# The closing phase of a fused attention and mixture-of-experts kernel: eight buffers, all loads issued at the start, four neighbouring tokens to a partition, the sum in place

## The chip, the cores and the metric

The kernel runs on one core of one Trainium2 chip. The metric is the device time of one execution in microseconds (us), the median of several. A core has four compute engines that matter here: TensorE (PE, matrix products), VectorE (DVE), ScalarE (ACT) and GpSimd (POOL). SyncE (SP) issues most of the transfers, which 16 DMA engines carry out between the large memory (DRAM) and the on-chip memory of 128 partitions (SBUF). Engines run on their own and wait for each other at semaphores: an instruction or a finished transfer raises one, and another engine waits until it has a given value. All data is float32.

## The reference

Only the last lines matter for the change. `D` is 256; there are 2 x 2048 = 4096 tokens.

```python
def _layernorm(x, axis=-1, eps=1e-05):
    m = jnp.mean(x, axis=axis, keepdims=True)
    v = jnp.var(x, axis=axis, keepdims=True)
    return (x - m) / jnp.sqrt(v + eps)
...
    x = L0_attn_x
    x = _layernorm(x + _L0_attn_ref(x, ...), axis=-1)   # gated delta rule over 16 heads
    x = _layernorm(x + _L0_ffn_ref(x, ...), axis=-1)    # 6 of 64 experts, and a shared one
    return x
```

## The kernel before

The program is a row of phases, each a block of its own with a barrier at its end: `gates_phase` and `delta_phase` (the attention), `mix_phase` (output projection, first normalisation, routing, the shared expert), `expert_phase` (64 experts), and `combine_phase`, the only one that the diff touches.

The experts' results stand in two DRAM tensors, `acc[0]` and `acc[1]`, each of 128 + 4096 rows of 256 numbers. The first 128 rows are for unused slots; the other rows belong to the tokens. `acc[0]` starts from the residual plus the shared expert's output; the even experts add into `acc[0]` and the odd ones into `acc[1]`. `combine_phase` computes, for each token, the sum of its two rows and the normalisation of that sum, and stores it to `out`. It moves 2 x 4 MiB in and 4 MiB out.

It works in eight groups (`GROUPS` = 8) of 512 tokens. For each group:

- SP loads the group's rows of `acc[0]` into `first` and of `acc[1]` into `second` (lines 1432 and 1433), 512 KB each. In SBUF a group is 128 partitions x 1024 numbers.
- DVE adds the two (line 1452) and takes mean and variance of each token (`bn_stats`, line 1455, and `bn_aggr`, line 1458, four of each, since a partition holds four tokens).
- POOL makes from these the scale and the shift in four small operations on 128 x 4 numbers (lines 1467, 1469, 1470 and 1473; line 1469 is a power of -1/2, called the power operation below).
- ACT applies them, four activations of 128 x 256 (line 1483), into `res`.
- SP stores `res` (line 1441).

Each of `first`, `second`, `total` and `res` has two buffers; group `g` uses number `g % 2`. So DVE waits with group `g` until ACT has finished group `g - 2` (`done`), ACT waits until the store of group `g - 2` has landed (`stored`), and SP issues the loads of group `g + 2` only when DVE has summed group `g` (`summed`). SP's own order is written out by hand: the loads of groups 0 and 1; then for each group `g` the loads of group `g + 2`, and after them the wait for `done` of group `g` and its store. The loads of a later group thus stand behind the store, and behind the wait, of an earlier one.

`rows` sets which tokens a partition holds: token `g*512 + k*128 + p` in place `k` of partition `p`. A transfer of a group is 512 runs of 1 KB.

`gates_phase`, at the program's start, has transfers of the two kinds that the change makes: it loads its input in eight pieces of 128 partitions x 1024 numbers, runs of 4 KB, each with a semaphore of its own (`gates_xs`, line 82), for the first of which TensorE waits (line 121); and it stores zeros to `acc[1]` in runs of 8.25 KB (line 95).

`s.w13`, named by the change, is the on-chip store for expert weights (28 x 704 numbers on a partition), last read by `expert_phase`.

Of the kernel before, what the change touches and what calls it, by code (L numbers as in the profile page):

```python
# [15 lines left out]
NTILE = NTOK // 128  # L16
# [14 lines left out]
EPS = 1e-5  # L31
# [1377 lines left out]
def combine_phase(nc, a, s, out):  # L1409

    sem = s.sem
    with ExitStack() as own:  # L1412
        def two(name, cols):
            return [own.enter_context(nc.sbuf_tensor(f"combine_{name}{i}", [128, cols], F32)) for i in range(2)]

        first, second, total, res = two("first", 1024), two("second", 1024), two("total", 1024), two("res", 1024)
        st, mv, rstd, shift = two("st", 24), two("mv", 8), two("rstd", 4), two("shift", 4)
        loaded, stored = [sem(f"c_loaded{i}") for i in range(2)], [sem(f"c_stored{i}") for i in range(2)]
        summed, st_out, mv_out, eps, power, mean, shifted, done = (
            sem(f"c_{n}") for n in ("summed", "st_out", "mv_out", "eps", "power", "mean", "shifted", "done"))  # L1420
        GROUPS = NTILE // 4
# [24 lines left out]
        def _(ve):  # L1446
            for g in range(GROUPS):
                e = g % 2
                ve.wait_ge(loaded[e], 32 * (g // 2 + 1))
                if g >= 2:  # L1450
                    ve.wait_ge(done, 4 * (g - 1))
                ve.tensor_tensor(total[e][:, :], first[e][:, :], second[e][:, :], ALU.add).then_inc(summed, 1)  # L1452
                ve.wait_ge(summed, g + 1)
                for k in range(4):
                    ve.bn_stats(st[e][:, k * 6:k * 6 + 6], total[e][:, k * D:k * D + D]).then_inc(st_out, 1)  # L1455
                for k in range(4):
                    ve.wait_ge(st_out, 4 * g + k + 1)
                    ve.bn_aggr(mv[e][:, k * 2:k * 2 + 2], st[e][:, k * 6:k * 6 + 6]).then_inc(mv_out, 1)  # L1458

        @block.gpsimd  # L1460
        def _(po):
            for g in range(GROUPS):
                e = g % 2
# [3 lines left out]
                po.tensor_scalar(rstd[e][:, :], view(mv[e], 1, (2, 4)), EPS, None, ALU.add).then_inc(eps, 1)  # L1467
                po.wait_ge(eps, g + 1)
                po.tensor_tensor(rstd[e][:, :], rstd[e][:, :], view(s.minus_half, 0, (0, 4)), ALU.pow).then_inc(power, 1)  # L1469
                po.tensor_scalar(shift[e][:, :], view(mv[e], 0, (2, 4)), -1.0, None, ALU.mult).then_inc(mean, 1)  # L1470
                po.wait_ge(power, g + 1)
                po.wait_ge(mean, g + 1)
                po.tensor_tensor(shift[e][:, :], shift[e][:, :], rstd[e][:, :], ALU.mult).then_inc(shifted, 1)  # L1473

        @block.scalar
        def _(ac):
            for g in range(GROUPS):
                e = g % 2
                ac.wait_ge(shifted, g + 1)
                if g >= 2:  # L1480
                    ac.wait_ge(stored[e], 16 * (g // 2))
                for k in range(4):
                    ac.activation(res[e][:, k * D:k * D + D], total[e][:, k * D:k * D + D], ACT.Identity,  # L1483
                                  bias=shift[e][:, k:k + 1], scale=rstd[e][:, k:k + 1]).then_inc(done, 1)


def program(nc, a, out):
    with ExitStack() as ctx:
# [32 lines left out]
        mix_phase(nc, a, s)  # L1521
        expert_phase(nc, a, s)
        combine_phase(nc, a, s, out)


# [89 lines left out]
```

## Time and profile before

| | |
|---|---|
| Time, median of 3 runs | 1837.96 us (1837.03 to 1841.89) |
| The profiled execution's own time | 1834.91 us |
| Its span, first to last instruction | 1833.0 us |
| Busy over the span | PE 88%, DVE 65%, ACT 50%, POOL 47% |
| `combine_phase` in it | from 1781.46 us (first load issued) to 1833.0 us |
| Busy from 1781 to 1833 us | DVE 23.28, ACT 16.58, POOL 15.99, PE 0 us |
| DMA in that stretch | 12.58 MB, mean 242 GB/s, engines busy 74% |

The shares of the whole span are those of the long phases before. For the change only the last 52 us count: there no engine is busy for even half of the time, and the DMA engines for three quarters of it. Lines of the trace give a start in us from the span's start and a duration; `[... <-X]` says how long the engine sat idle before and what ended that.

### The profile page before, as it was taken

What the parts mean: (1) busy time and instruction counts of PE and PEld (TensorE: products, weight loads), DVE (VectorE), ACT (ScalarE), POOL (GpSimd) and SP (SyncE); (2) the same over time, 40 slices, a digit from 0 to 9 for tenths busy, and PEclk for the clock granted to TensorE, in tenths of its full rate; (3) what the DMA queues carried; (4) which work ended last, traced back from release to release, by engine and by line L of the source; (5) the groups of instructions that cost most, each with busy time, mean ns of one, the idle gap of its engine ahead of it and who ended that gap; (6) DMA issues with size and microseconds to landing.
All of it is one profiled execution on the core that took longest, in us unless ns stands there. A gap on an engine that the chain in (4) does not pass through costs nothing. (4 is left out here: it accounts for less than half of the span.)

```text
span 1833.0 us, 74029 instructions
## 1 busy us (share of the span) xinstructions
PE 1616.1 (88%) x31244; PEld 1234.2 (67%) x31244; DVE 1194.4 (65%) x3029; ACT 909.6 (50%) x2314; POOL 865.8 (47%) x1133
## 2 busy tenths in 40 slices
PE   7479999999999999999999999759999994899950
PEld 6136666666676666667667666658888884878840
DVE  1378888888888888888888888514555553222215
ACT  1266766676676666666666666311222221333313
POOL 0034344344344344344344344214777776677853
PEclk9799999999999999999999999879999998899985
DMA  6235455556555555555555555434555551799557
GB/s 272 81 80 119 113 115 121 126 113 124 126 114 121 126 114 122 126 113 123 126 113 122 115 115 118 80 106 149 176 153 176 153 153 35 203 262 223 93 93 244
DMA packets 530218, 245.45 MB, mean 134 GB/s; under 512 B 423504, under 2 KB 497872, under 8 KB 528992
## 3 DMA queue, kind: packets, MB, share of 16 engines
q1 hardware_dynamic: 377824, 200.75, 42.1%
q10 hardware_dynamic: 133632, 20.98, 6.1%
q0 software_dynamic: 18432, 18.99, 5.9%
q8 instruction: 247, 4.05, 1.0%
q14 instruction: 83, 0.68, 0.1%
HBM read 169.29 MB, written 71.37 MB: 131 GB/s over the span
## 5 line engine op out<-in xcount | busy, mean ns | idle before, releaser
L375 PE MATMUL delta_p_j<-delta_xt,delta_w 128*128 128x512 f32 x768 | 386.2, 626 | 31.4 <-DMA delta_xt<-in_xt 17.5
L575 DVE SCALAR_TENSOR_TENSOR delta_kq<-delta_hist,cw,delta_kq 128x512 f32<-128x512 f32 x384 | 295.6, 770 | 30.7 <-ACT delta_kq L723 23.7
L716 ACT ACTIVATE delta_hist<-delta_p_j 128x512 f32<-128x512 f32 x192 | 114.8, 598 | 251.9 <-PE delta_p_j L375 248.0
L889 POOL TENSOR_TENSOR delta_sd<-state,eg_end 128x256 f32<-128x256 f32 x128 | 104.4, 815 | 283.2 <-DVE state L655 283.2
L375 PEld LDWEIGHTS delta_p_j<-delta_xt,delta_w 128*128 128x128 f32 x768 | 131.5, 191 | 146.6 <-issue 111.9
L1248 POOL DMA_INDIRECT slot_tokens<-mix_tokens,mix_slot x192 | 190.2, 990 | 62.4 <-issue 61.8
L436 PEld LDWEIGHTS delta_p_i<-delta_kkq,rt 64*64 64x64 f32 x4096 | 130.3, 135 | 73.1 <-DVE delta_kkq L639 67.9
L864 POOL TENSOR_SCALAR delta_n<-delta_n 128x8 f32<-128x8 f32 x64 | 15.5, 242 | 296.7 <-DVE delta_n L606 296.7
L436 PE MATMUL delta_p_i<-delta_kkq,rt 64*64 64x32 f32 (+1 forms) x4096 | 143.3, 214 | 13.9 <-DVE delta_kkq L639 13.5
L1371 DVE SCALAR_TENSOR_TENSOR expert_gate<-expert_gate,expert_p_h 88x256 f32<-88x256 f32 x64 | 26.7, 417 | 174.7 <-ACT expert_gate L1391 174.7
L589 DVE SCALAR_TENSOR_TENSOR delta_yv<-delta_hist,cw,delta_yv 128x512 f32<-128x512 f32 x128 | 132.5, 1035 | 8.1 <-ACT delta_yv L723 5.9
L1342 PE MATMUL expert_p_h<-expert_xbt,w 128*88 128x128 f32 x1024 | 127.3, 278 | 9.9 <-ACT expert_xbt L1385 9.0
L779 ACT ACTIVATE delta_kpv<-delta_kpv,delta_root 128x64 f32<-128x64 f32 x512 | 135.4, 346 | 0.0
L1342 PEld LDWEIGHTS expert_p_h<-expert_xbt,w 128*88 128x88 f32 x1024 | 115.6, 158 | 29.2 <-ACT expert_xbt L1385 27.5
L883 POOL TENSOR_TENSOR delta_root<-delta_n,half_power 128x8 f32<-128x8 f32 x64 | 133.9, 2093 | 0.0
L495 PEld LDWEIGHTS delta_p_c<-delta_r,delta_kkq 64*64 64x64 f32 x2048 | 71.0, 136 | 92.4 <-issue 86.4
L1036 PE MATMUL mix_p_y<-mix_wo,mix_ot 128*128 128x256 f32 x512 | 117.9, 384 | 14.8 <-DMA mix_wo<-in_wo 14.8
L773 ACT ACTIVATE delta_kpv<-delta_kpv,delta_fk 128x64 f32<-128x64 f32 x512 | 128.8, 343 | 0.5 <-POOL delta_fk L871 0.5
L647 DVE TENSOR_TENSOR delta_r<-delta_kpv,delta_p_c 128x256 f32<-128x256 f32 x128 | 53.8, 420 | 98.1 <-PE delta_p_c L470 97.1
L1310 POOL DMA_INDIRECT acc<-expert_yb,expert_tokens x64 | 100.6, 1572 | 32.2 <-ACT expert_yb L1397 17.7
L1036 PEld LDWEIGHTS mix_p_y<-mix_wo,mix_ot 128*128 128x128 f32 x512 | 96.2, 193 | 27.0 <-issue 14.9
L632 DVE TENSOR_TENSOR delta_xi<-delta_xi,delta_outer 128x15 f32<-128x15 f32 (+7 forms) x480 | 99.0, 206 | 16.4
(145 smaller groups left out, 3641.4 us busy)
## 6 DMA issues: line engine op xcount, KB each, us to landing
delta_xd<-x_scratch SPq DMA_DIRECT2D x256, 128.0 KB, 4.3
delta_w<-in_wqkv SPq DMA_DIRECT2D x64, 416.0 KB
w<-in_w SPq DMA_DIRECT2D x64, 352.0 KB
delta_eg<-eg_rows SPq DMA_DIRECT2D x128, 130.0 KB
n_scratch<-delta_kkq ACTq DMA_DIRECT2D x128, 128.0 KB
mix_ot<-ot SPq DMA_DIRECT2D x16, 1024.0 KB, 5.7
w<-in_w SPq DMA_DIRECT2D x64, 176.0 KB
ot<-delta_o SPq DMA_DIRECT2D x32, 256.0 KB
```

The source lines that it names most:

```text
L375: mm = pe.matmul(p_j[:, :], w[e][:, (ch * 3 + n) * 128:(ch * 3 + n) * 128 + 128], xt[m // 8 % 2][:, ch * 512:ch * 512 + 512], start=ch == ...
L436: mm = pe.matmul(view(p_i, g * C + first, (1, count), parts=half(sh)), view(lhs, g * C, (1, C), parts=half(sh)), view(rhs, at + g * C + fi ...
L575: ve.scalar_tensor_tensor(out, view(hist[e], i * 2 * 518 + tap, (259, 2), (1, 256)), cw[:, column:column + 1], out, ALU.mult, ALU.add).the ...
L589: ve.scalar_tensor_tensor(out, view(hist[e], 518 + tap, (259, 2), (1, 256)), cw[:, column:column + 1], out, ALU.mult, ALU.add).then_inc(co ...
L716: ac.activation(view(hist[e], n * 518 + 3, (259, 2), (1, 256)), p_j[:, :], ACT.Copy)
L773: ac.activation(kpv[:, at:at + C], kpv[:, at:at + C], ACT.Copy, scale=fk[:, g:g + 1]).then_inc(kp_out, 1)
L779: ac.activation(kpv[:, at:at + C], kpv[:, at:at + C], ACT.Copy, scale=root[:, g:g + 1]).then_inc(vp_out, 1)
L883: po.tensor_tensor(root[:, :], n2[:, :], view(s.half_power, 0, (0, 8)), ALU.pow).then_inc(small, 1)
L889: po.tensor_tensor(view(sd, 0, (128, 2), (C, 2), (1, C)), view(state, first_pair(group) * 128, (C, 2), (128, 2), (1, C)), view(s.eg_end, g ...
L1036: mm = pe.matmul(p_y[i % 2][:, 0:D], ot[i // 2 % 2][:, p * 256 + i % 2 * 128:p * 256 + i % 2 * 128 + 128], wo[:, p * D:p * D + D], start=p ...
L1248: po.indirect_dma_start(out=s.tok.ap(), out_offset=bass.IndirectOffsetOnAxis(ap=slot[i % 2][:, k:k + 1], axis=0), in_=tokens[:, i:i + 1], ...
L1342: mm = pe.matmul(p_h[e % 2][0:HALF, piece * 128:piece * 128 + 128], s.w13[:, at * 704 + ch * SI + piece * HALF:at * 704 + ch * SI + piece ...
```

## The change

Every group has a place of its own, so nothing is reused within the phase. Eight stretches of `s.w13` take the loads of `acc[0]` and then the sums (`total`). Eight `res` buffers take the loads of `acc[1]` and, once the sum is made, the results. DVE adds in place. `first` and `second` are gone, and with them the waits for `summed` (SP), `done` (DVE and POOL) and `stored` (ACT). SP issues all 16 loads first and then the eight stores, each behind its wait. `rows` now puts tokens `g*512 + 4p` to `g*512 + 4p + 3` on partition `p`, so that a transfer is 128 runs of 4 KB.

```diff
-        first, second, total, res = two("first", 1024), two("second", 1024), two("total", 1024), two("res", 1024)
-        st, mv, rstd, shift = two("st", 24), two("mv", 8), two("rstd", 4), two("shift", 4)
-        loaded, stored = [sem(f"c_loaded{i}") for i in range(2)], [sem(f"c_stored{i}") for i in range(2)]
+        total, res = [s.w13[:, g * 1024:g * 1024 + 1024] for g in range(GROUPS)], each("res", 1024)
+        st, mv, rstd, shift = each("st", 24), each("mv", 8), each("rstd", 4), each("shift", 4)
+        loaded, stored = [sem(f"c_loaded{i}") for i in range(GROUPS)], sem("c_stored")
...
         def rows(t, g, skip):
-            return bass.AP(t, (g * 4 + skip) * 128 * D, [[D, 128], [128 * D, 4], [1, D]])
+            return bass.AP(t, (g * 4 + skip) * 128 * D, [[4 * D, 128], [1, 4 * D]])
...
-            def load(g):
-                if g >= 2:
-                    sp.wait_ge(summed, g - 1)
-                sp.dma_start(view(first[g % 2], 0, (D, 4), (1, D)), rows(s.acc[0], g, 1)).then_inc(loaded[g % 2], 16)
-                sp.dma_start(view(second[g % 2], 0, (D, 4), (1, D)), rows(s.acc[1], g, 1)).then_inc(loaded[g % 2], 16)
-
-            load(0)
-            load(1)
             for g in range(GROUPS):
-                if g + 2 < GROUPS:
-                    load(g + 2)
+                sp.dma_start(total[g], rows(s.acc[0], g, 1)).then_inc(loaded[g], 16)
+                sp.dma_start(res[g][:, :], rows(s.acc[1], g, 1)).then_inc(loaded[g], 16)
+            for g in range(GROUPS):
                 sp.wait_ge(done, 4 * g + 4)
-                sp.dma_start(rows(out, g, 0), view(res[g % 2], 0, (D, 4), (1, D))).then_inc(stored[g % 2], 16)
-            for i in range(2):
-                sp.wait_ge(stored[i], 16 * GROUPS // 2)
+                sp.dma_start(rows(out, g, 0), res[g][:, :]).then_inc(stored, 16)
+            sp.wait_ge(stored, 16 * GROUPS)
...
-                e = g % 2
-                ve.wait_ge(loaded[e], 32 * (g // 2 + 1))
-                if g >= 2:
-                    ve.wait_ge(done, 4 * (g - 1))
-                ve.tensor_tensor(total[e][:, :], first[e][:, :], second[e][:, :], ALU.add).then_inc(summed, 1)
+                ve.wait_ge(loaded[g], 32)
+                ve.tensor_tensor(total[g], total[g], res[g][:, :], ALU.add).then_inc(summed, 1)
...
                 po.wait_ge(mv_out, 4 * g + 4)
-                if g >= 2:
-                    po.wait_ge(done, 4 * (g - 1))
...
                 ac.wait_ge(shifted, g + 1)
-                if g >= 2:
-                    ac.wait_ge(stored[e], 16 * (g // 2))
```

POOL's and ACT's operations are otherwise the same, on `[g]` in place of `[e]`.

On SP's queue, at the start of the phase, this is the order of the transfers with the semaphores that each waits for (`c_summed` is DVE's sum, `c_done` ACT's last activation; `w` is the stretch of `s.w13`):

```order
-L1432 DMA combine_first<-acc 128x4x256
-L1433 DMA combine_second<-acc 128x4x256
-L1432 DMA combine_first<-acc 128x4x256
-L1433 DMA combine_second<-acc 128x4x256
-L1432 DMA combine_first<-acc 128x4x256 [waits c_summed]
-L1433 DMA combine_second<-acc 128x4x256
-L1441 DMA out<-combine_res 128x4x256 [waits c_done]
...
+L1431 DMA w<-acc 128x1024
+L1432 DMA combine_res<-acc 128x1024
...
+L1435 DMA out<-combine_res 128x1024 [waits c_done] x8
```

The pair of loads in the new order stands eight times, with no wait and no store between; the stores, which stood between the loads, have moved behind the last load.

On DVE, from the third group on (group 2), this is the sum and the statistics, before and now:

```order
-L1452 TENSOR_TENSOR combine_total<-combine_first,combine_second 128x1024 [waits c_done,c_loaded0]
-L1455 BN_STATS combine_st<-combine_total 128x6 [waits c_summed]
-L1455 BN_STATS combine_st<-combine_total 128x6 x3
-L1458 BN_AGGR combine_mv<-combine_st 128x2 [waits c_st_out] x4
...
+L1442 TENSOR_TENSOR w<-w,combine_res 128x1024 [waits c_loaded2]
+L1445 BN_STATS combine_st<-w 128x6 [waits c_summed]
+L1445 BN_STATS combine_st<-w 128x6 x3
+L1448 BN_AGGR combine_mv<-combine_st 128x2 [waits c_st_out] x4
```

The operations and their shapes stand as they were; the wait for ACT (`c_done`) is gone, and the load has a semaphore of its own.

## Rows read from the trace of the kernel before

**Rows 1.** Busy time by stretch: time, engines busy, TensorE clock, DMA share, GB/s.

```profile
1781.00:1833.00 52.00, 0.00 (x0) 0.00 (x0) 23.28 (x72) 16.58 (x32) 15.99 (x32) 0.50 0.74 242
```

**Rows 2.** The group of DVE's sums, from 1781 us: busy, mean ns, idle before and releasers.

```profile
L1452 DVE TENSOR_TENSOR combine_total<-combine_first,combine_second 128x1024 f32<-128x1024 f32 x8 | 9.8, 1225 | 35.0 <-DMA combine_second<-acc 29.9 <-ACT combine_res L1483 5.2
```

**Rows 3.** Chain that ended last, in order of time, from 1781 us.

```profile
1782.98 7.84 DMA combine_second<-acc
...
1799.50 7.93 DMA combine_second<-acc
...
1816.35 5.83 DMA combine_second<-acc
```

**Rows 4.** DVE in order of time, from 1781 us.

```profile
1787.37 1.22 DVE L1452 TENSOR_TENSOR combine_total<-combine_first,combine_second 128x1024 f32<-128x1024 f32 x1 [20.80 <-DMA combine_second<-acc]
...
1789.95 0.36 DVE L1458 BATCH_NORM_AGGREGATE combine_mv<-combine_st 128x2 f32<-128x6 f32 x4
1790.84 1.22 DVE L1452 TENSOR_TENSOR combine_total<-combine_first,combine_second 128x1024 f32<-128x1024 f32 x1 [0.52 <-DMA combine_second<-acc]
...
1794.72 1.23 DVE L1452 TENSOR_TENSOR combine_total<-combine_first,combine_second 128x1024 f32<-128x1024 f32 x1 [0.94 <-ACT combine_res L1483]
...
1811.57 1.23 DVE L1452 TENSOR_TENSOR combine_total<-combine_first,combine_second 128x1024 f32<-128x1024 f32 x1 [1.18 <-DMA combine_second<-acc]
...
1816.39 1.23 DVE L1452 TENSOR_TENSOR combine_total<-combine_first,combine_second 128x1024 f32<-128x1024 f32 x1 [1.88 <-DMA combine_second<-acc]
...
1822.20 1.22 DVE L1452 TENSOR_TENSOR combine_total<-combine_first,combine_second 128x1024 f32<-128x1024 f32 x1 [2.87 <-DMA combine_second<-acc]
...
1824.79 0.36 DVE L1458 BATCH_NORM_AGGREGATE combine_mv<-combine_st 128x2 f32<-128x6 f32 x4
```

**Rows 5.** POOL in order of time, from 1781 us.

```profile
1790.41 0.24 POOL L1467 TENSOR_SCALAR combine_rstd<-combine_mv 128x4 f32<-128x4 f32 x1 [15.29 <-DVE combine_mv L1458]
1790.73 1.05 POOL L1469 TENSOR_TENSOR combine_rstd<-combine_rstd,minus_half 128x4 f32<-128x4 f32 x1
...
1795.31 0.73 POOL L1470 TENSOR_SCALAR combine_shift<-combine_mv 128x4 f32<-128x4 f32 x1
...
1816.42 1.25 POOL L1473 TENSOR_TENSOR combine_shift<-combine_shift,combine_rstd 128x4 f32<-128x4 f32 x1
```

**Rows 6.** SP's transfers in order of time, and the stores' first and last start.

```profile
1781.46 0.38 SPq L1432 DMA_DIRECT2D combine_first<-acc  x1
...
1788.62 0.36 SPq L1432 DMA_DIRECT2D combine_first<-acc  x1
...
L1441 SPq DMA_DIRECT2D out<-combine_res x8: 372/378/378, 1794.6 to 1829.4; - x8
```

**Rows 7.** Busy time by single microseconds (columns as in Rows 1).

```profile
1782.00:1783.00 1.00, 0.00 (x0) 0.00 (x0) 0.00 (x0) 0.00 (x0) 0.00 (x0) 0.50 0.23 38
...
1789.00:1790.00 1.00, 0.00 (x0) 0.00 (x0) 1.00 (x5) 0.00 (x0) 0.00 (x0) 0.50 0.40 114
...
1794.00:1795.00 1.00, 0.00 (x0) 0.00 (x0) 0.28 (x1) 0.62 (x2) 0.92 (x2) 0.50 0.00 0
...
1806.00:1807.00 1.00, 0.00 (x0) 0.00 (x0) 0.00 (x0) 0.02 (x1) 0.71 (x3) 0.50 1.09 385
...
1817.00:1818.00 1.00, 0.00 (x0) 0.00 (x0) 0.96 (x3) 0.29 (x1) 0.67 (x1) 0.50 1.02 264
```

**Rows 8.** Busy time by stretch: steady loads and stores here, and two stretches of `gates_phase`.

```profile
1798.00:1809.00 11.00, 0.00 (x0) 0.00 (x0) 4.43 (x11) 4.59 (x10) 3.18 (x7) 0.50 1.04 361
10.00:15.00 5.00, 5.00 (x99) 5.00 (x98) 0.00 (x0) 0.00 (x0) 0.00 (x0) 1.00 1.02 412
25.00:30.00 5.00, 5.00 (x98) 5.00 (x98) 0.00 (x0) 0.00 (x0) 0.00 (x0) 1.00 1.03 419
```

**Rows 9.** Transfers of `gates_phase`: count, ns min/median/max, first and last start; who waited.

```profile
L82 SPq DMA_DIRECT2D gates_xs<-in_xt x8: 420/474/847, 1.2 to 6.2; - x8
...
  PE gates_p_z L121: 5.1, 1
```

More of the change, by code:

```diff
@@ L1412, in combine_phase @@
     with ExitStack() as own:
-        def two(name, cols):
-            return [own.enter_context(nc.sbuf_tensor(f"combine_{name}{i}", [128, cols], F32)) for i in range(2)]
-        first, second, total, res = two("first", 1024), two("second", 1024), two("total", 1024), two("res", 1024)
-        st, mv, rstd, shift = two("st", 24), two("mv", 8), two("rstd", 4), two("shift", 4)
-        loaded, stored = [sem(f"c_loaded{i}") for i in range(2)], [sem(f"c_stored{i}") for i in range(2)]
+        GROUPS = NTILE // 4
@@ L1419, in combine_phase, with each @@
+        def each(name, cols):
+            return [own.enter_context(nc.sbuf_tensor(f"combine_{name}{i}", [128, cols], F32)) for i in range(GROUPS)]
+        total, res = [s.w13[:, g * 1024:g * 1024 + 1024] for g in range(GROUPS)], each("res", 1024)
+        st, mv, rstd, shift = each("st", 24), each("mv", 8), each("rstd", 4), each("shift", 4)
+        loaded, stored = [sem(f"c_loaded{i}") for i in range(GROUPS)], sem("c_stored")
         summed, st_out, mv_out, eps, power, mean, shifted, done = (
@@ L1447, in _ @@
             for g in range(GROUPS):
-                e = g % 2
-                ve.wait_ge(loaded[e], 32 * (g // 2 + 1))
-                if g >= 2:
-                    ve.wait_ge(done, 4 * (g - 1))
-                ve.tensor_tensor(total[e][:, :], first[e][:, :], second[e][:, :], ALU.add).then_inc(summed, 1)
+                ve.wait_ge(loaded[g], 32)
+                ve.tensor_tensor(total[g], total[g], res[g][:, :], ALU.add).then_inc(summed, 1)
                 ve.wait_ge(summed, g + 1)
                 for k in range(4):
-                    ve.bn_stats(st[e][:, k * 6:k * 6 + 6], total[e][:, k * D:k * D + D]).then_inc(st_out, 1)
+                    ve.bn_stats(st[g][:, k * 6:k * 6 + 6], total[g][:, k * D:k * D + D]).then_inc(st_out, 1)
                 for k in range(4):
                     ve.wait_ge(st_out, 4 * g + k + 1)
-                    ve.bn_aggr(mv[e][:, k * 2:k * 2 + 2], st[e][:, k * 6:k * 6 + 6]).then_inc(mv_out, 1)
+                    ve.bn_aggr(mv[g][:, k * 2:k * 2 + 2], st[g][:, k * 6:k * 6 + 6]).then_inc(mv_out, 1)
         @block.gpsimd
@@ L1462, in _ @@
             for g in range(GROUPS):
-                e = g % 2
                 po.wait_ge(mv_out, 4 * g + 4)
-                if g >= 2:
-                    po.wait_ge(done, 4 * (g - 1))
-                po.tensor_scalar(rstd[e][:, :], view(mv[e], 1, (2, 4)), EPS, None, ALU.add).then_inc(eps, 1)
+                po.tensor_scalar(rstd[g][:, :], view(mv[g], 1, (2, 4)), EPS, None, ALU.add).then_inc(eps, 1)
                 po.wait_ge(eps, g + 1)
-                po.tensor_tensor(rstd[e][:, :], rstd[e][:, :], view(s.minus_half, 0, (0, 4)), ALU.pow).then_inc(power, 1)
-                po.tensor_scalar(shift[e][:, :], view(mv[e], 0, (2, 4)), -1.0, None, ALU.mult).then_inc(mean, 1)
+                po.tensor_tensor(rstd[g][:, :], rstd[g][:, :], view(s.minus_half, 0, (0, 4)), ALU.pow).then_inc(power, 1)
+                po.tensor_scalar(shift[g][:, :], view(mv[g], 0, (2, 4)), -1.0, None, ALU.mult).then_inc(mean, 1)
                 po.wait_ge(power, g + 1)
                 po.wait_ge(mean, g + 1)
-                po.tensor_tensor(shift[e][:, :], shift[e][:, :], rstd[e][:, :], ALU.mult).then_inc(shifted, 1)
+                po.tensor_tensor(shift[g][:, :], shift[g][:, :], rstd[g][:, :], ALU.mult).then_inc(shifted, 1)
         @block.scalar
@@ L1477, in _ @@
             for g in range(GROUPS):
-                e = g % 2
                 ac.wait_ge(shifted, g + 1)
-                if g >= 2:
-                    ac.wait_ge(stored[e], 16 * (g // 2))
                 for k in range(4):
-                    ac.activation(res[e][:, k * D:k * D + D], total[e][:, k * D:k * D + D], ACT.Identity,
-                                  bias=shift[e][:, k:k + 1], scale=rstd[e][:, k:k + 1]).then_inc(done, 1)
+                    ac.activation(res[g][:, k * D:k * D + D], total[g][:, k * D:k * D + D], ACT.Identity,
+                                  bias=shift[g][:, k:k + 1], scale=rstd[g][:, k:k + 1]).then_inc(done, 1)
 def program(nc, a, out):
```

1 line of the change is left out of this document (removed).

## The prediction

> **What bounds the kernel now.** I read the stretches first: from 1781 us to the end TensorE does nothing, DVE works 23.28 of 52 us, ACT 16.58 and POOL 15.99, and the DMA engines are busy 74% of the time at a mean of 242 GB/s [rows 1]. No engine is full, so the phase is held by waits. Next comes who waits: DVE's eight sums stood idle 35.0 us before they could start, 29.9 of it for the load of `second` and 5.2 for ACT to free the sum's buffer [rows 2]. The chain of work that ended last says the same: three stretches of 7.84, 7.93 and 5.83 us, 21.6 of its 52 us, in which it stands in a load of `second` [rows 3].
>
> Those loads are late because they are issued late, not only because DMA is slow. After the first four, SP issues the next at 1788.62, when the first sum is made [rows 6]; the DMA engines have by then nearly run dry (114 GB/s between 1789 and 1790), and between 1794 and 1795 they move nothing at all [rows 7]. Full stretches reach 385 GB/s, and the best eleven microseconds average 361, loads and stores together [rows 7, 8]. At 361 the 12.58 MB would take 34.8 us; the phase takes 51.5.
>
> **What the change leaves as the limit.** The removed waits make three streams independent, and each is to be costed; the slowest sets the end.
>
> DVE's stream. One group takes from the sum's start at 1787.37 to the end of its last `bn_aggr` at 1789.95 + 0.36 = 1790.31, which is 2.94 us; the sum of group 1 was then waited for 0.52 us, so it could start 0.01 to 0.03 us after [rows 4]. I take 2.97 us for each group. Eight groups are 23.7 us of work without a gap, where DVE's groups now start 34.83 us apart, first to last (1787.37 to 1822.20) [rows 4]. The sum in place has the same two inputs and 1024 columns, and its cost stays 1.22 us.
>
> The first start. Data begins to flow about 1782.8 (the engines are 23% busy between 1782 and 1783) and the first sum starts at 1787.37 [rows 4, 7]. Group 1's data ends near 1789.4 and its sum starts at 1790.84, so a landing takes about 1.4 us to be seen [rows 4, 7]. That leaves some 3.15 us for group 0's 1.05 MB, about 333 GB/s with the run-up. Loads with runs of 4 KB are in the trace: `gates_phase` at 412 GB/s over five microseconds, and stores with longer runs at 419 [rows 8]. At 412 the 1.05 MB takes 2.55 us. I credit 0.4 of the 0.6 us, since the run-up stays: start at 1787.0.
>
> The loads' stream. At 412 GB/s a group lands every 2.55 us, the last at 1782.8 + 20.4 + 1.4 = 1804.6; at 361 every 2.90 us, the last at 1807.4. DVE wants it at 1787.0 + 7 x 2.97 = 1807.8. So DVE, not the loads, is the pace, down to about 355 GB/s. SP needs 0.47 us for such an issue [rows 9], 16 are 8 us, done near 1789.5; the first store is wanted only at 1787.0 + 7.3 = 1794.3 (sum's start to store's start, 1787.37 to 1794.6 [rows 4, 6]). Moving the stores behind 16 loads on SP's queue is thus free in issue. On the DMA engines, though, the stores of groups 0 to 3 stand behind the loads until 1803.2: four of 0.52 MB at 385 GB/s are 5.4 us, and with the next two the queue is empty near 1811. The last store, wanted at 1815, finds it free. Nothing on chip waits for the earlier ones, since `stored` no longer holds ACT.
>
> ACT and POOL. ACT's 16.58 and POOL's 15.99 us of work over eight groups are 2.07 and 2.0 us for each, under 2.97 [rows 1]. But POOL's operations will now meet DVE's sum every time. Where one started during a sum, it ended with it: the shift multiplication started at 1816.42, took 1.25 us and ended 0.05 us after the sum that ran 1816.39 to 1817.62; the operation at 1795.31 took 0.73 us and ended at 1796.04, 0.09 after a sum [rows 4, 5]. Now POOL's first operation comes 0.10 us after the last `bn_aggr` [rows 4, 5], just behind the next group's sum, and will be held about 1.2 us. The four operations, some 2.1 us with gaps, then end 3.1 us after `bn_aggr`, 0.15 more than DVE's period. Only the last group counts, and no sum follows it: it pays for POOL's backlog of 0.1 us, or up to 0.8 if the fourth operation is held as well. DVE does not wait for POOL anywhere. I take 0.1.
>
> The reverse, POOL holding DVE, does not show: the sum at 1790.84 began while the power operation (1790.73, 1.05 us) ran, and took its usual 1.22 [rows 4, 5]. The Trainium skill (SBUF — State Buffer, Who interferes with whom) says that whichever issues first holds the port pair for the whole instruction and the other blocks fully, for a DVE instruction with two SBUF inputs against a POOL one that reads SBUF. The first half agrees with this trace, the second does not; by the rule alone the sum would gain up to 0.1 us a group where the fourth operation gets in just ahead, and the end would move by some 0.8 us.
>
> The tail. From the last `bn_aggr`'s end (1824.79 + 0.36 = 1825.15) to the span's end at 1833.0 are 7.85 us [rows 4]: POOL, ACT, the last store. It stays, runs of 4 KB or not; the last store starts at 1829.4 and is 3.6 us of it [rows 6].
>
> **The sum.** 1787.0 + 7 x 2.97 + 2.94 + 7.85 + 0.1 = 1818.7, against 1833.0: 14.3 us less. The profiled execution took 1834.91 us, so it would take 1820.6. The median of the runs shown is 3.05 us above that execution; taken off the median the prediction is 1837.96 - 14.3 = 1823.7 us, 0.8% less. Everything ahead of 1781 us is unchanged and costs nothing either way.
>
> **Rivals.** (A) *The DMA stream is the limit.* All 12.58 MB then flow without a gap but slower than 355 GB/s. For it: where stores and loads mix now, the engines were full at 264 GB/s between 1817 and 1818 [rows 7], and over the whole phase the rate per busy time is 242 / 0.74 = 327. Against it: the changed order mixes them only at one seam, and runs are longer. At 327 the flow takes 38.5 us and ends at 1782.8 + 38.5 + 1.4 = 1822.7, so 1827.7 us in the median.
>
> (B) *POOL holds DVE after all.* If each power operation of 1.04 us stopped the next sum, seven times, the end would be 7.3 us later: 1831.0. The sum at 1790.84 speaks against it, with one more pair alike; POOL's place against DVE will differ, though.
>
> (C) *Hardly anything.* A saving below 5.5 us, which is 0.3% and about what a measurement of this kernel can tell from no change, needs an end after 1827.5, so a stream under 12.58 / 43.3 = 290 GB/s throughout. Only mixed microseconds are that low now.
>
> (D) *Slower, through the order in which transfers are served.* With 16 loads in flight the engines might share themselves among all, so that group 0 lands with the last. Then nothing overlaps: at 361 GB/s the first sum starts at 1807.4, the last at 1828.2, and the end is 1828.2 + 2.94 + 7.85 = 1839.0, 6.0 us later: 1844.0 us. It decides for slower below about 370 GB/s; at 412 the end is 1836.2, within 0.3%. Against it: with four loads in flight, group 0's sum started 3.47 us before group 1's [rows 4], and TensorE got its first 4 KB-run piece at 5.1 us, when SP was still issuing the eighth (to 6.2) [rows 9]. The Trainium skill (DMA: Bandwidth & Descriptors, Queues, rings and completion order) states that on each engine descriptors are consumed in ring order, though completions may differ; that too makes this unlikely.
>
> **How the numbers follow.** Chances: DVE as the pace 0.62, A 0.20, B 0.08, C 0.06, D 0.04. The forecast is 1823.7, with its own range 1822 to 1825.5 from the first start (0.4 us either way), POOL's backlog (to 0.8) and the runs' spread. The range of 1820 to 1829 adds A down to about 315 GB/s and part of B; below, it leaves room for a median as low against the rows as the profiled run was. Faster by over 0.3%: all of the forecast, A and B, 0.90. Within: C and the half of D at high rates, 0.08. Slower: 0.02.
>
> **What the profile after would show.** Right: sums about 2.97 us apart with no idle time before them after the first; DMA near 400 GB/s without a gap from 1783 to about 1803; the stores of groups 0 to 3 landing late, the last in some 3.5 us; POOL's first operation of each group stretched to about 1.4 us, the last group's not; a span of about 1818.7. Wrong: idle time before the sums released by loads (A, or D if it is all before the first); sums that start late or last over 1.23 us while POOL works (B); DMA rates under 290 (C).

## The result, and the profile after

The changed kernel takes 1821.55 us (median of 6 runs, 1819.7 to 1832.13) against 1838.81 us (median of 6, 1831.2 to 1841.89). The ratio is 0.9914 with a 95% interval of 0.9889 to 0.9939: 0.86% faster, where 0.78% and 1823.7 us were forecast.

The profiled execution of the changed kernel is one of its long ones: 1832.13 us, with a span of 1830.3 us, only 2.7 us under the 1833.0 of before. Its last phase does not begin until 1793.54 us, 12.1 us later than in the trace of before [rows 6], although nothing ahead of it was changed (more on this at the end of the part on the prediction). So the phase is compared by its own length, from SP's first load to the end of the span:

| | before | after |
|---|---|---|
| First load issued, us | 1781.46 | 1793.54 |
| First sum, after that | 5.91 | 5.37 |
| First sum to last sum | 34.83 | 20.07 |
| Last sum to the last store's issue | 7.20 | 7.93 |
| From there to the end of the span | 3.60 | 3.40 |
| Length of the phase | 51.5 | 36.8 |

The phase is 14.8 us shorter, 0.8% of the kernel; the interval of the ratio is 11 to 20 us, and holds it.

SP's transfers after the change, in order of time, and the group of the stores:

```profile
1793.54 0.33 SPq L1431 DMA_DIRECT2D w<-acc  x1
...
1801.88 1.72 SPq L1432 DMA_DIRECT2D combine_res<-acc  x1
1806.95 20.32 SPq L1435 DMA_DIRECT2D out<-combine_res  x8
...
L1435 SPq DMA_DIRECT2D out<-combine_res x8: 332/332/338, 1806.9 to 1826.9; - x8
```

The 16 loads go out within 10.1 us (1793.54 to 1803.6), where before the change the third pair of loads alone stood 7.2 us behind the first [rows 6]. DVE after the change, in order of time:

```profile
1798.91 1.22 DVE L1442 TENSOR_TENSOR w<-w,combine_res 128x1024 f32<-128x1024 f32 x1 [20.43 <-DMA combine_res<-acc]
...
1801.96 1.25 DVE L1442 TENSOR_TENSOR w<-w,combine_res 128x1024 f32<-128x1024 f32 x1
...
1804.84 1.19 DVE L1442 TENSOR_TENSOR w<-w,combine_res 128x1024 f32<-128x1024 f32 x1
...
1807.66 1.19 DVE L1442 TENSOR_TENSOR w<-w,combine_res 128x1024 f32<-128x1024 f32 x1
...
1813.32 1.20 DVE L1442 TENSOR_TENSOR w<-w,combine_res 128x1024 f32<-128x1024 f32 x1
...
1818.98 1.20 DVE L1442 TENSOR_TENSOR w<-w,combine_res 128x1024 f32<-128x1024 f32 x1
...
1821.53 0.36 DVE L1448 BATCH_NORM_AGGREGATE combine_mv<-combine_st 128x2 f32<-128x6 f32 x4
```

Only the first sum shows a wait for its load here. The second comes 3.05 us after it and is held a little by its load as well; the chain that ended last still runs through it:

```profile
1794.85 7.08 DMA combine_res<-acc
```

From the third on the sums stand 2.83 us apart, where the seven steps had averaged 4.98 us (34.83 in all, [rows 4]). Who waited for whom, from 1775 us on (total us, times, longest):

```profile
DVE w L1442 <- DMA combine_res<-acc: 20.4, 1, 20.4
```

That 20.4 us is the wait for the first load, most of it in the phase before, while the experts' last results were still being added. The 35.0 us of waits before the sums [rows 2] held 20.8 us of the same kind; what the change could remove were the other 14.2 us, and they are gone. The DMA engines, in single microseconds (columns as in Rows 1):

```profile
1796.00:1797.00 1.00, 0.00 (x0) 0.00 (x0) 0.00 (x0) 0.00 (x0) 0.00 (x0) 0.50 1.01 406
...
1804.00:1805.00 1.00, 0.00 (x0) 0.00 (x0) 1.00 (x7) 0.15 (x1) 0.57 (x3) 0.50 1.00 410
...
1821.00:1822.00 1.00, 0.00 (x0) 0.00 (x0) 0.89 (x6) 1.00 (x3) 1.00 (x1) 0.50 1.02 414
1822.00:1823.00 1.00, 0.00 (x0) 0.00 (x0) 0.00 (x0) 0.98 (x3) 0.68 (x4) 0.50 0.25 98
```

From 1796 to 1822 they are busy for 93% or more of every microsecond, at 332 to 442 GB/s: mostly under 390 in the first six microseconds, near 410 for most of the rest, first with loads and then with the stores that had gathered behind them. In between there is no microsecond at 0, 114 or 264 GB/s as in [rows 7]. POOL and ACT after the change:

```profile
1801.94 0.24 POOL L1454 TENSOR_SCALAR combine_rstd<-combine_mv 128x4 f32<-128x4 f32 x1 [14.87 <-DVE combine_mv L1448]
1802.27 1.85 POOL L1456 TENSOR_TENSOR combine_rstd<-combine_rstd,minus_half 128x4 f32<-128x4 f32 x1
...
1805.01 1.11 POOL L1454 TENSOR_SCALAR combine_rstd<-combine_mv 128x4 f32<-128x4 f32 x1 [0.20 <-DVE combine_mv L1448]
...
1807.72 1.19 POOL L1460 TENSOR_TENSOR combine_shift<-combine_shift,combine_rstd 128x4 f32<-128x4 f32 x1
...
1812.51 1.04 POOL L1456 TENSOR_TENSOR combine_rstd<-combine_rstd,minus_half 128x4 f32<-128x4 f32 x1
1813.63 0.97 POOL L1457 TENSOR_SCALAR combine_shift<-combine_mv 128x4 f32<-128x4 f32 x1
...
1822.79 0.23 POOL L1454 TENSOR_SCALAR combine_rstd<-combine_mv 128x4 f32<-128x4 f32 x1
...
1820.64 6.27 ACT L1467 ACTIVATE combine_res<-w,combine_shift,combine_rstd 128x256 f32<-128x256 f32 x12 [0.75 <-POOL combine_shift L1460]
```

In each of the first six groups one of POOL's four operations (in the second group two) meets a sum of DVE and is stretched: the power operation from 1.04 to 1.85 us, the others from 0.20 to 0.24 to between 0.97 and 1.35 us. POOL runs behind: its operations for the last group start at 1822.79, 0.90 us after the last `bn_aggr` ended (1821.53 + 0.36 = 1821.89), and ACT's last twelve activations follow each other without a gap.

### The profile page after: what moved, and what is told of

It reads as the page before. It is cut to its first block and busy times, and to the rows that moved or that the text cites. A ratio compares the mean times of both kernels' runs of the same rounds, so it can differ in the third digit from the quotient of the medians.

```text
span 1830.3 us, 74010 instructions
## 1 busy us (share of the span) xinstructions
PE 1620.1 (89%) x31244; PEld 1240.8 (68%) x31244; DVE 1194.0 (65%) x3029; ACT 909.9 (50%) x2314; POOL 870.2 (48%) x1133
## 5 line engine op out<-in xcount | busy, mean ns | idle before, releaser
L1310 POOL DMA_INDIRECT acc<-expert_yb,expert_tokens x64 | 100.5, 1571 | 36.5 <-ACT expert_yb L1397 20.2
```

## The experiments

Each run is told by the length of its last phase, since the time ahead of it varies: the first load of this phase was issued anywhere between 1781.5 and 1796.5 us in the 13 profiled executions. The length is read from one profiled execution of each run. The changed kernel was profiled twice, `after` and e8, and the two differ by 0.3 us, so differences of that size tell nothing by themselves. Timed runs have a ratio to the kernel before, measured on the same chip; those without a ratio (the first row aside) were executed once.

| Run | Phase, us | Starts of the sums, first to last, us | Ratio, 95% interval |
|---|---|---|---|
| before | 51.5 | 34.8 | |
| after | 36.8 | 20.1 | 0.9914 (0.9889 to 0.9939) |
| e1 rows only | 51.2 | 35.3 | 0.9993 (0.997 to 1.0016) |
| e2 places only | 38.1 | 21.0 | 0.9944 (0.9924 to 0.9964) |
| e3 old order | 51.0 | 35.4 | 1.0 (0.9983 to 1.0017) |
| e4 extra POOL operation | 36.8 | 19.8 | |
| e5 four ahead | 43.5 | 28.2 | |
| e6 stores on ACT | 45.3 | 28.9 | 0.9965 (0.9947 to 0.9983) |
| e7 short tail | 35.4 | 20.1 | 0.9907 (0.9879 to 0.9935) |
| e8 after again | 36.5 | 19.8 | 0.9918 (0.9888 to 0.9948) |
| e9 extra DVE operation | 38.2 | 22.1 | |
| e10 after, stores on ACT | 37.7 | 22.2 | |
| e11 four ahead, stores on ACT | 37.1 | 21.7 | |

### The rows alone (e1)

```diff
-            return bass.AP(t, (g * 4 + skip) * 128 * D, [[D, 128], [128 * D, 4], [1, D]])
+            return bass.AP(t, (g * 4 + skip) * 128 * D, [[4 * D, 128], [1, 4 * D]])
```

The SBUF side of the transfers is written as a plain 128 x 1024 buffer to go with it.

> The kernel before, with the one line changed that puts four neighbouring tokens on a partition (transfers of 128 runs of 4 KB); buffers, waits and order stay. Measured by the phase's length, from SP's first load to the span's end: 51.5 us before, 36.8 after the whole change. If late issue is the cost (my theory), faster data shortens only the flight of the loads that are waited for: 0.4 us at the start and about 0.5 us at each of some four waits, so 48.5 to 50 us, and the time within 0.3% of before. If the length of the runs is what gave the gain, the phase comes to 40 us or less and the time is 0.6% lower.

The phase takes 51.2 us (1789.00 to 1840.2), 0.3 less than before, under even the small gain that I expected, and no more than the two traces of one kernel differ. The wait for the load is not shorter; its rows in this run's list of waits, beside those of ACT's release:

```profile
DVE combine_total L1452 <- DMA combine_second<-acc: 32.1, 5, 20.6
DVE combine_total L1452 <- ACT combine_res L1483: 3.4, 2, 2.4
```

What faster data gave at one place it lost at another: the third group's load landed 1.5 us before its sum, which then stood 2.4 us for ACT to free the buffer, and from 1801 to 1803 the DMA engines moved nothing. Faster data in a queue that runs dry makes it run dry sooner.

### The places without the rows (e2)

The changed kernel with the old line of `rows` (the reverse of the diff above, SBUF side included).

> The changed kernel with the old rows (512 runs of 1 KB in each transfer). By my theory VectorE is the pace as long as loads flow at 355 GB/s, and 1 KB runs reached 361 to 385 in full stretches: the phase takes 37 to 38.5 us, 36.8 with long runs. The rival, that the DMA stream is the limit with short runs (327 GB/s on average before), gives idle time before the sums from the third group on and a phase of 41 to 43 us.

38.1 us, inside what I gave my theory, but with another reason. The engines at the steady part of the loads, and SP's issue of one load there:

```profile
1808.00:1810.00 2.00, 0.00 (x0) 0.00 (x0) 1.89 (x4) 1.74 (x4) 1.81 (x3) 0.50 1.10 350
1810.00:1812.00 2.00, 0.00 (x0) 0.00 (x0) 1.93 (x8) 1.10 (x3) 1.68 (x4) 0.50 1.09 346
```

```profile
1809.65 1.42 SPq L1431 DMA_DIRECT2D w<-acc  x1
```

With 1 KB runs the loads flow at 350 GB/s, a group in 3.00 us, and the sums stand 3.01 us apart: the DMA stream, not DVE, is the pace here, as rival A had it. The trace shows it directly too: each of the eight sums starts 0.02 us after its load of `acc[1]` has landed (the fourth at 1811.10, landed 1811.07), where in e8 from the third group on the loads lie 0.6 to 1.9 us ahead of their sums. From the sixth load on, SP's issue takes 1.25 to 1.87 us, mostly 1.42, instead of 0.5. With the 0.04 us to the next that is 512 KB at 359 GB/s, near the rate of the engines. So the long rows are worth 1.3 to 1.6 us when the loads are early (against `after` and e8), and 0.3 us or nothing when they are late (e1).

### Places and rows, but SP's old order (e3)

```diff
+            def load(g):
+                if g >= 2:
+                    sp.wait_ge(summed, g - 1)
+                sp.dma_start(total[g], rows(s.acc[0], g, 1)).then_inc(loaded[g], 16)
+                sp.dma_start(res[g][:, :], rows(s.acc[1], g, 1)).then_inc(loaded[g], 16)
+
+            load(0)
+            load(1)
             for g in range(GROUPS):
-                sp.dma_start(total[g], rows(s.acc[0], g, 1)).then_inc(loaded[g], 16)
-                sp.dma_start(res[g][:, :], rows(s.acc[1], g, 1)).then_inc(loaded[g], 16)
-            for g in range(GROUPS):
+                if g + 2 < GROUPS:
+                    load(g + 2)
                 sp.wait_ge(done, 4 * g + 4)
```

> The changed kernel with its eight places and 4 KB runs, but SP's old order and wait: the loads of group g+2 wait for the sum of g and stand behind the store of g-1. If the order in which the loads are issued is what mattered, load g+3 goes out only after the last activation of g, about 7 us after its sum, needs 4.5 us to land, and three groups pass in some 12 us: about 4 us a group and a phase of 43 to 46 us. If the reuse of the buffers (the waits for done and stored) was the cost, this stays at 37 to 38 us.

51.0 us, and a ratio of 1.0: eight places and 4 KB runs with the old order give 0.5 us in the trace and nothing that the times can show. It is longer than the 43 to 46 us of my estimate. SP's queue around the first store, and who waited before the sums:

```profile
1792.07 0.43 SPq L1434 DMA_DIRECT2D combine_res<-acc  x1
1798.64 0.34 SPq L1442 DMA_DIRECT2D out<-combine_res  x1
1799.02 0.43 SPq L1433 DMA_DIRECT2D w<-acc  x1
```

```profile
DVE w L1449 <- DMA combine_res<-acc: 35.2, 7, 20.4
```

SP stands from 1792.5 to 1798.64 at the wait for group 0's result, and the load of group 3, free to go since the second sum (over at 1794.6), goes out only at 1799.02; its sum comes at 1806.10. Two terms of my estimate were too small: group 0's result came 8.2 us after its sum, not 7, and the load, with a store beside it, took 6.6 us to land (its second half from 1799.49 to 1806.08), not 4.5. Under the old order the reuse of buffers had cost next to nothing by itself. With a place for every group, the order is worth 14.2 us (51.0 to 36.8).

### The order alone, otherwise the kernel before (e6)

```diff
-                sp.wait_ge(done, 4 * g + 4)
-                sp.dma_start(rows(out, g, 0), view(res[g % 2], 0, (D, 4), (1, D))).then_inc(stored[g % 2], 16)
...
+                ac.wait_ge(done, 4 * g + 4)
+                ac.dma_start(rows(out, g, 0), view(res[e], 0, (D, 4), (1, D))).then_inc(stored[e], 16)
```

The two added lines stand on ACT, behind a group's four activations.

> The kernel before, with two buffers and 1 KB runs, where ScalarE issues the stores after its own activations, so that on SP's queue no load stands behind a wait for a result. If that order was the cost, load g+2 goes out at the sum of g; the sum of g+2 then waits for the last activation of g, 7.3 us after its sum: 3.7 us a group and a phase of 42 to 43.5 us against 51.5, the time 0.4 to 0.5% lower. If the two buffers are the cost, the phase stays above 48 us.

45.3 us: 6.2 us of the 14.8 come from two moved lines, with two buffers and 1 KB runs, and the kernel is measurably faster (0.9965). The rest needs the places too. The waits left in this run from 1795 us on, behind the first sum:

```profile
DVE combine_total L1450 <- DMA combine_second<-acc: 6.5, 5, 1.7
DVE combine_total L1450 <- ACT combine_res L1481: 1.9, 2, 0.9
```

That is between the two numbers, nearer to the first. The first three steps from sum to sum are 3.9 us, near what the two buffers allow; the later ones are 3.9 to 4.6, and five of the sums wait for a load. So order and places are not a sum of two gains: places give 0.5 us under the old order (e3, with the rows), the order 6.2 with two buffers, both 14.8 with the rows.

### How far ahead (e5 and e11)

In e5 SP issues four groups first and every later load behind a store; e11 is the same depth, but the loads wait only for a sum and ACT issues the stores.

```diff
-            for g in range(GROUPS):
+            for g in range(4):
                 sp.dma_start(total[g], rows(s.acc[0], g, 1)).then_inc(loaded[g], 16)
                 sp.dma_start(res[g][:, :], rows(s.acc[1], g, 1)).then_inc(loaded[g], 16)
             for g in range(GROUPS):
                 sp.wait_ge(done, 4 * g + 4)
                 sp.dma_start(rows(out, g, 0), res[g][:, :]).then_inc(stored, 16)
+                if g + 4 < GROUPS:
+                    sp.dma_start(total[g + 4], rows(s.acc[0], g + 4, 1)).then_inc(loaded[g + 4], 16)
+                    sp.dma_start(res[g + 4][:, :], rows(s.acc[1], g + 4, 1)).then_inc(loaded[g + 4], 16)
```

> The changed kernel, but SP issues only the loads of groups 0 to 3 first; those of group g+4 stand behind the store of group g. If what counts is how far ahead a load is issued, group g+4 is asked for about 7.3 us after the sum of g, lands 4.5 to 5.5 us later, and its sum comes 12 to 13 us after that of g, where VectorE's own pace would give 11.3: a phase of 37.5 to 39.5 us. If any load behind a store's wait costs what the old order cost, the phase is 43 us or more.

> The four-ahead kernel with no load behind a store's wait: SP issues the loads of groups 0 to 3, then those of group g+4 at the sum of g, and ScalarE issues the stores. Each load goes out 10 us ahead of its sum and needs 4 to 6. If the wait in SP's order was what made the four-ahead kernel slow (43.5 us), this takes 36.5 to 38.5 us, with what mixed stores cost on top as in the run beside it; if fewer loads in flight were the cost, it stays at 42 us or more.

e5 takes 43.5 us, not 37.5 to 39.5: my estimate from how far ahead a load goes out fell, and the run gave the rival's number. SP and the engines in that run:

```profile
1792.56 0.44 SPq L1432 DMA_DIRECT2D combine_res<-acc  x1
1803.23 0.34 SPq L1435 DMA_DIRECT2D out<-combine_res  x1
1803.61 0.43 SPq L1437 DMA_DIRECT2D w<-acc  x1
```

```profile
1798.00:1800.00 2.00, 0.00 (x0) 0.00 (x0) 1.97 (x10) 0.00 (x0) 1.67 (x4) 0.50 1.02 418
1800.00:1802.00 2.00, 0.00 (x0) 0.00 (x0) 1.97 (x4) 0.87 (x2) 1.83 (x3) 0.50 0.49 197
1802.00:1804.00 2.00, 0.00 (x0) 0.00 (x0) 1.97 (x8) 1.20 (x3) 1.86 (x2) 0.50 0.00 0
1804.00:1806.00 2.00, 0.00 (x0) 0.00 (x0) 1.58 (x8) 1.67 (x4) 1.65 (x4) 0.50 0.97 315
```

Again two terms were too small. Group 0's result was ready 9.1 us after its sum (1794.15 to 1803.23), not 7.3, because POOL's first and fourth operation are held by the next two sums (1.12 and 1.16 us); and the restart is dear: between 1802 and 1804 nothing moves, then store and loads of 1.57 MB share the queue, and group 4's sum comes at 1809.70, 7.03 us after group 3's. The last two sums are 3.8 us apart, which is 1.57 MB at 415 GB/s: from there on the DMA stream is the pace, and what it lost while it stood idle is not made up. e11, with the same depth and the wait out of the loads' way, takes 37.1 us. It still has a wait on SP, for the sum of four groups before, and that one costs nothing that shows beside e10 (37.7). So it is not the number of loads in flight that counts, but that no load waits behind a result.

### What is the pace now (e4 and e9)

e4 adds an operation to POOL in each group, e9 one to DVE:

```diff
+                po.tensor_scalar(spare[g][:, :], view(mv[g], 0, (2, 4)), -1.0, None, ALU.mult)
                 po.tensor_scalar(rstd[g][:, :], view(mv[g], 1, (2, 4)), EPS, None, ALU.add).then_inc(eps, 1)
```

```diff
+                ve.bn_stats(spare[g][:, :], total[g][:, 0:D])
                 for k in range(4):
                     ve.bn_stats(st[g][:, k * 6:k * 6 + 6], total[g][:, k * D:k * D + D]).then_inc(st_out, 1)
```

> The changed kernel with one more small operation of GpSimd in each group (128 x 4, about 0.24 us and 0.08 us of gap), ahead of the four. After the change the chain that ended last runs through GpSimd from the second group on. If GpSimd is the pace, each group takes 0.32 us more and the phase grows by 2.2 to 2.6 us, to 39 to 39.4. If VectorE is the pace and GpSimd is only held by VectorE's sums (0.73 us of each group), the hold shrinks by what is added, groups stay 2.83 us apart, and only the last two groups show it: 0.3 to 0.7 us, a phase of 37.1 to 37.5 us.

> The changed kernel with one more bn_stats of VectorE in each group (128 x 256, some 0.33 us between the starts of two), its result unused. If VectorE is the pace of the phase, the sums stand 3.16 us apart instead of 2.83 and the phase grows by eight times 0.33, to 39.0 to 39.6 us. If loads or GpSimd are the pace, VectorE has slack and the phase stays under 37.5 us.

e4 takes 36.8 us. Its sums run over the same 19.8 us as those of e8 (36.5 us), so the operation cost 0.3 us at most, no more than two traces of one kernel differ and the low end of the 0.3 to 0.7 expected; the trace of `after` (36.8 us) had lost 0.2 us to its second load. POOL in one group of e4:

```profile
1811.28 0.22 POOL L1454 TENSOR_SCALAR combine_spare<-combine_mv 128x4 f32<-128x4 f32 x1
1811.57 0.23 POOL L1455 TENSOR_SCALAR combine_rstd<-combine_mv 128x4 f32<-128x4 f32 x1
1811.88 1.04 POOL L1457 TENSOR_TENSOR combine_rstd<-combine_rstd,minus_half 128x4 f32<-128x4 f32 x1
1813.00 0.80 POOL L1458 TENSOR_SCALAR combine_shift<-combine_mv 128x4 f32<-128x4 f32 x1
1813.95 0.20 POOL L1461 TENSOR_TENSOR combine_shift<-combine_shift,combine_rstd 128x4 f32<-128x4 f32 x1
```

The held operation shrank from 0.97 to 0.80 us, the gaps between operations took the rest, and the sums stayed 2.83 us apart. The chain that ended last runs through POOL after the change, and POOL is still not the pace; that chain follows a backlog. In e9 the sums move:

```profile
1806.34 1.19 DVE L1442 TENSOR_TENSOR w<-w,combine_res 128x1024 f32<-128x1024 f32 x1
...
1809.49 1.19 DVE L1442 TENSOR_TENSOR w<-w,combine_res 128x1024 f32<-128x1024 f32 x1
```

They are 3.15 us apart, 0.32 more, which is what DVE as the pace gives: the loads land as before, the last 3.7 us ahead of its sum, and POOL waits for DVE in every group. The phase grew by 1.4 us to 38.2 (1.7 against e8), less than the 2.2 to 2.8 expected: POOL, with more time in each group, keeps up, and the last `bn_aggr` to the end of the span takes 7.57 us (1819.03 to 1826.6) instead of 8.41. An experiment that slows one engine gave back another's backlog.

### Stores among the loads (e10)

ACT issues the stores, as in e6, in the changed kernel; SP issues only the 16 loads.

> The changed kernel with the stores issued by ScalarE, on its own queue, so that they no longer stand behind the 16 loads but move among them. In the four-ahead run the engines moved 315 to 379 GB/s while loads and stores were in flight together, and 416 when only one kind was. If mixing costs rate, the loads slow down from the first store on, the sums of the last groups wait for loads, and the phase takes 38 to 41 us. If it does not, nothing is lost by it and the phase stays at 36.3 to 37.1 us.

37.7 us, between the two expectations. The engines around the first stores (issued from 1799.2 on):

```profile
1798.00:1800.00 2.00, 0.00 (x0) 0.00 (x0) 1.97 (x8) 1.13 (x3) 1.80 (x2) 0.50 1.03 416
1800.00:1802.00 2.00, 0.00 (x0) 0.00 (x0) 2.00 (x9) 1.74 (x4) 1.72 (x4) 0.50 1.04 389
1802.00:1804.00 2.00, 0.00 (x0) 0.00 (x0) 1.97 (x6) 1.25 (x3) 1.69 (x4) 0.50 0.99 352
1804.00:1806.00 2.00, 0.00 (x0) 0.00 (x0) 1.97 (x8) 1.25 (x4) 1.68 (x4) 0.50 1.02 418
```

The rate dips for four microseconds and is back at 418 to 426 GB/s with both kinds in flight. The last two sums do wait (3.9 to 4.0 us apart), but because the stores take their share of the same bytes a second. So the loss of 0.9 us (1.2 against e8) seems to be displacement more than a lower rate; the dip is about 0.4 us of it (166 KB fewer than at 412 GB/s), and the 315 to 379 GB/s of e5 is not explained by the mixture alone; its cause stays open. That the stores stand behind all loads is worth about 1 us here, since nobody waits for an early store.

### A shorter end (e7, with e8 as its measure)

DVE's part; POOL and ACT leave out what it takes over, and SP waits for both:

```diff
+                if g >= GROUPS - 2:
+                    ve.wait_ge(mv_out, 4 * g + 4)
+                    ve.tensor_scalar(rstd[g][:, :], view(mv[g], 1, (2, 4)), EPS, None, ALU.add).then_inc(ready_ve, 1)
+                    ve.tensor_scalar(shift[g][:, :], view(mv[g], 0, (2, 4)), -1.0, None, ALU.mult).then_inc(ready_ve, 1)
+            for g in (GROUPS - 2, GROUPS - 1):
+                ve.wait_ge(shifted, g + 1)
+                for k in range(2 if g == GROUPS - 2 else 1, 4):
+                    ve.tensor_scalar(res[g][:, k * D:k * D + D], total[g][:, k * D:k * D + D], rstd[g][:, k:k + 1],
+                                     shift[g][:, k:k + 1], ALU.mult, ALU.add).then_inc(done_ve, 1)
```

> The changed kernel with a shorter end: VectorE, which is free after the last bn_aggr, makes two of GpSimd's four small operations of the last two groups, and applies scale and shift to two of the four tokens of group 6 and three of the four of group 7. From the last bn_aggr to the last store's issue there were 5.06 us, 0.8 of it GpSimd's backlog and 2.07 ScalarE's four activations. Expected: backlog gone, two operations less, 1.2 us less at the apply: 1.5 to 2.5 us, a phase of 34.5 to 35.5 us. If the store queue or ScalarE's own backlog sets the end, under 0.5 us is gained.

> The changed kernel once more, as the measure for the run beside it and for how much the stages ahead of the last phase vary. The phase again takes 36.5 to 37.1 us; the first load goes out anywhere between 1781 and 1797 us, as in the profiled executions so far.

e7 takes 35.4 us, e8 36.5. The phase is in the range that was expected, the gain is not quite: 1.1 us against its neighbour and 1.4 against the first trace of the changed kernel, where 1.5 to 2.5 was expected. DVE's part of e7's last group:

```profile
1816.23 0.36 DVE L1451 BATCH_NORM_AGGREGATE combine_mv<-combine_st 128x2 f32<-128x6 f32 x4
...
1818.35 1.06 DVE L1459 TENSOR_SCALAR combine_res<-w,combine_rstd,combine_shift 128x256 f32<-128x256 f32 x3 [0.85 <-POOL combine_shift L1475]
```

From the last `bn_aggr` to the last store's issue it is now 2.9 us (1816.59 to 1819.5) instead of 5.06. But the end of the span follows 4.2 us after that issue instead of 3.4: the store of group 6 has gone out only 1.1 us earlier (1818.43) and probably stands in the way. The timed ratios, 0.9907 and 0.9918, can't tell the two apart; the traces can. It is the shortest phase of all that ran.

## Why the prediction was right, step by step

The phase was forecast at 37.2 us (1781.46 to 1818.7) and took 36.8 (36.5 in e8). The median was forecast at 1823.7 us and is 1821.55, in the range of 1820 to 1829 but under the forecast's own range of 1822 to 1825.5. The phase explains 14.8 of the 17.3 us between the medians; the other 2.5 us are not in the phase and lie within the spread of the stages ahead (below): that the median is so low is luck of the runs. By its own terms:

- *The waits, not the engines, were the limit, and the loads late because issued late.* Right, and e1 and e3 sharpen it: neither faster transfers nor more places help while SP's list holds the loads back.
- *5.2 us of waits for ACT to free the sum's buffer* [rows 2]. Misread: 0.94 us. The other 4.22 us stand before the fourth sum, which needs ACT's work on group 1 only:

```profile
1796.42 2.07 ACT L1483 ACTIVATE combine_res<-combine_total,combine_shift,combine_rstd 128x256 f32<-128x256 f32 x4 [1.80 <-POOL combine_shift L1473]
...
1801.89 1.23 DVE L1452 TENSOR_TENSOR combine_total<-combine_first,combine_second 128x1024 f32<-128x1024 f32 x1 [4.22 <-ACT combine_res L1483]
```

  ACT was done with group 1 at 1798.49. The fourth group's load landed at 1801.87, and ACT's last activation of group 2 happened to end at 1801.88. So this wait, too, was for a load, and that fits e3, where the places alone gave so little. No term of the sum rests on the 5.2 us.
- *First sum at 5.5 us after the first load.* 5.37.
- *2.97 us for a group of DVE.* 2.83 from the third sum on, and 20.07 us for the seven instead of 20.79: the largest error in the good direction. A sum that does not wait starts while the last `bn_aggr` is still recorded (1807.39 + 0.36 = 1807.75, next sum at 1807.66), and lasts 1.19 instead of 1.22 us.
- *DVE is the pace, down to 355 GB/s.* The pace is right, as e9 shows. The turning point was put too low: with 2.83 us for a group DVE takes its 1.05 MB at about 370 GB/s, so the loads become the pace below that. And loads with 1 KB runs are slower than the 361 to 385 GB/s that the prediction and the expectation of e2 read from stretches with stores in them. Loads alone had run at 331 to 359 GB/s in the trace of before (1784 to 1788), and e2's ran at 345 to 356.
- *SP issues the 16 loads in 8 us.* 10.1 us, and 9.6 in e8. Nobody waited for it: group 0's store was wanted only at 1806.95.
- *The tail of 7.85 us plus 0.1 for POOL's backlog.* Mis-sized: 8.41 us. POOL's first operation for the last group starts 0.90 us after the last `bn_aggr`, where it started 0.10 after [rows 4, 5], so the backlog is 0.8 us, the upper bound that the prediction gave and set aside. The last store was 0.2 us quicker. The errors, 0.7 us down for the pace, 0.2 down for the start and 0.5 up here, leave 0.5 us: the sum is closer than its terms, because they partly cancel.
- *POOL's first operation of each group is the one held.* Right for one group only, the second (1805.01, 1.11 us), where the fourth was held as well; in group 0 it was the power operation. A group with its first operation held takes POOL longer than DVE's 2.83 us, as the prediction itself had it (3.1 us), so the meeting moved on, to the fourth operation and then to the third, where it settled (1813.63, 0.97 us). In e8 the first operation of group 0 was held and the power operation was not, and the meeting moved in the same way.
- *POOL does not hold DVE* (against rival B). Right: the sums last 1.19 to 1.25 us. The 1.25 is the one at 1801.96 that started 0.02 us after a POOL operation; the last sum of e2 did the same (1823.05, after POOL's at 1823.03) and lasted 1.25 too. That is all there is of the reverse. The Trainium skill (SBUF — State Buffer, Who interferes with whom) calls the shared port pair an exclusive lock, with the issue order deciding who blocks; its words on the whole instruction stand at another mode of DVE, and the prediction carried them over. Here a sum started 0.81 us into the power operation (1813.32, with POOL's at 1812.51) and lasted 1.20.
- *Order of service* (rival D). With 16 loads in flight, the first sum came no later than before. The stores of the first groups landed late, the longest in 11.5 us, and nobody waited for them.

The profiled execution was forecast at 1820.6 us and took 1832.13. That is not the phase but its start, 12.1 us later. The last of the attention's state updates (line 889) started at 1225.0 instead of 1218.9 us, the first gather of the experts (line 1303) at 1568.2 instead of 1560.5, and the last addition (line 1310) at 1785.5 instead of 1773.6, so all three long phases gave some. It lies within the spread between executions: e8, the same program, began the phase at 1787.93, and all 13 profiled executions, with nothing changed ahead of it, between 1781.46 and 1796.52. It goes with TensorE's granted clock: the two long ones of the six timed runs (1831.28 and 1832.13 us) have a mean of 0.955 and 0.956 of full speed over the span, the four short ones (1819.7 to 1821.68 us) 0.959 to 0.963. What lowers it was not tried. The prediction, made from differences, was not touched by it, but it compared two executions as if they began alike.

## What to carry to other kernels

A queue that issues both loads and stores by hand is a list of waits: put nothing that needs only memory behind something that needs a result. Here that one rule was worth 6 us with two moved lines, more buffers without it were worth 0.5, and both together, with the long rows, 14.8. A releaser in a list of waits is an inference: check against the program which group it has to be. Once DMA has run dry in a phase whose pace is the DMA stream, the bytes lost are not made up (e5); so look first for intervals of 0 GB/s, and then for the entry of the queue that stood there. When one wait is gone, cost the next pace (here DVE, 2.83 us a group, with the loads at 2.55 just below), and the backlog of whoever is off the path but ends last.

## What the runs showed of the hardware

- A POOL operation on 128 x 4 numbers, other than the power operation, that starts during DVE's sum of two SBUF tensors ends 0.06 to 0.1 us after it: 0.20 to 0.24 us became up to 1.27 (e2). One that had started 0.07 us before the sum was held as well, 1.35 us (1810.42). The power operation, 1.04 us otherwise, took 1.85 when it started during a sum, and ended 0.91 us after it.
- The reverse did not happen with the power operation: sums that started during it lasted 1.19 to 1.20 us, in three of three groups.
- SP's issue of a 512 KB transfer took 0.43 us with 128 runs and 0.50 with 512 while few were in flight. With 512 runs it rose to 1.42 us each for most of e2's loads. With 128 runs the loads went out at 0.33 to 0.97 us each, and only the last of the 16 took longer (1.72 us, and 2.04 in e8).
- Loads with runs of 1 KB held 345 to 356 GB/s (e2), with 4 KB 406 to 426 once under way (`after`, from 1802 us on); stores alone 384 to 386 with 1 KB (e2) and 416 to 420 with 4 KB (e8).
